# A transformer's three one-unit cross attentions: order of VectorE's steps and of one ScalarE copy in a unit

## What is computed

```python
x = x + _L0_xattn_ref(_layernorm(x), ctx_512, ...)    # cross attention, 16 heads of 8
x = x + _L0_ffn_ref(_layernorm(x), ...)               # experts
x = x + _L1_xattn_ref(_layernorm(x), ctx_512, ...)    # causal self attention + cross attention
x = x + _L1_ffn_ref(_layernorm(x), ...)               # experts
x = x + _L2_xattn_ref(_layernorm(x), ctx_512, ...)    # two attentions with 16 heads of 32
x = x + _L2_ffn_ref(_layernorm(x), ...)               # experts
x = x + _L3_xattn_ref(_layernorm(x), ctx_512, ...)    # cross attention, 16 heads of 8
x = x + _L3_ffn_ref(_layernorm(x), ...)               # ternary MLP
```

```python
q, k, v = layernorm(x) @ Wq, ctx @ Wk, ctx @ Wv       # 256 queries, 64 keys, 16 heads of 8
x = x + (softmax(q @ k.T / sqrt(8)) @ v) @ Wo + bo
```

## Time and profile before

| | |
|---|---|
| median of 3 runs | 2486.17 us (2484.84 to 2491.94) |
| the profiled execution, device time | 2488.64 us |
| its span, first to last instruction | 2486.9 us |
| PE busy | 2136.2 us, 86% |
| PEld busy (weight load) | 1629.6 us, 66% |
| DVE busy | 1824.4 us, 73% |
| ACT busy | 1335.7 us, 54% |
| POOL busy | 1247.5 us, 50% |
| mean granted TensorE clock | 0.946 |

### The profile page before, as it was taken

One profiled execution on the slowest core, in us unless ns is written; L12 is line 12 of the kernel. 1 busy time (PEld: TensorE's weight loads), 2 busy tenths in 40 slices (PEclk: granted clock), 3 DMA queues, 4 the chain that ended last, 5 costly groups with the idle time before them and its releaser, 6 DMA issues. The chain is left out here.

```text
span 2486.9 us, 67321 instructions
## 1 busy us (share of the span) xinstructions
PE 2136.2 (86%) x22352; PEld 1629.6 (66%) x22352; DVE 1824.4 (73%) x4650; ACT 1335.7 (54%) x2821; POOL 1247.5 (50%) x1940
## 2 busy tenths in 40 slices
PE   5878997999988779599999997899789999998755
PEld 4557995556656568466666666666567888875523
DVE  5975554666659766489999968688698866667887
ACT  2444552444434456355555547355468888873466
POOL 4547635555535366477777745333264343334333
PEclk9978998999999879799999999899999999999978
DMA  8022211000000223200000000000000312210000
GB/s 307 20 112 76 78 53 30 16 13 14 11 2 1 83 76 105 62 13 11 9 9 11 8 2 21 10 1 0 19 5 2 103 56 67 56 43 15 1 11 24
DMA packets 82031, 96.69 MB, mean 39 GB/s; under 512 B 16720, under 2 KB 61136, under 8 KB 79760
## 3 DMA queue, kind: packets, MB, share of 16 engines
q1 hardware_dynamic: 73616, 77.12, 9.9%
q0 software_dynamic: 8192, 16.79, 2.3%
HBM read 56.51 MB, written 37.36 MB: 38 GB/s over the span
## 5 line engine op out<-in xcount | busy, mean ns | idle before, releaser
L1722 DVE TENSOR_TENSOR l2f_h_lo<-l2f_h,l2f_h_hi 128x512 fp32r<-128x512 f32 x256 | 187.1, 763 | 101.1 <-ACT l2f_h_hi L1643 101.0
L1012 POOL TENSOR_TENSOR a_pm<-a_pt,tri_post 128x256 f32<-128x256 f32 x256 | 179.6, 731 | 71.8 <-ACT a_pt L668 71.4
L1650 ACT ACTIVATE l2f_h<-l2f_f,ahead 128x512 f32<-128x512 f32 x256 | 174.2, 688 | 49.6 <-DVE l2f_h_lo L1722 32.5
L808 DVE TENSOR_REDUCE l1s_negm<-l1s_s 128x6 bf16<-128x768 f32 x128 | 123.1, 961 | 95.7 <-PE l1s_s L485 95.5
L1817 POOL TENSOR_TENSOR l2f_acc<-l2f_tmp,l2f_acc 128x512 f32<-128x512 f32 x56 | 73.0, 1303 | 207.2 <-DVE l2f_tmp L1740 207.2
L668 ACT ACTIVATE l1s_pt<-l1s_st 128x768 f32<-128x768 f32 x128 | 96.9, 812 | 144.9 <-PE l1s_st L523 144.9
L808 DVE TENSOR_REDUCE a_negm<-a_s 128x4 bf16<-128x1024 f32 x128 | 156.2, 1220 | 23.2 <-PE a_s L485 23.1
L1643 ACT ACTIVATE l2f_h_hi<-l2f_h 128x512 fp32r<-128x512 f32 x256 | 154.4, 633 | 0.0
L668 ACT ACTIVATE a_pt<-a_st 128x1024 f32<-128x1024 f32 x128 | 126.6, 1066 | 3.3 <-PE a_st L523 3.3
L684 ACT ACTIVATE a_q_hi<-a_pa 128x256 bf16<-128x256 f32 x64 | 24.5, 383 | 184.7 <-PE a_pa L451 184.7
L1534 PE MATMUL l2f_f<-l2f_x_hi,l2f_w_hi 128*128 128x512 f32 x256 | 101.7, 397 | 1.2 <-POOL l2f_w_lo L1804 1.2
(11 more groups left out here) (575 smaller groups left out, 6930.1 us busy)
## 6 DMA issues: line engine op xcount, KB each, us to landing
expert_rows<-zeros SPq DMA_DIRECT2D x16, 1056.0 KB, 17.5
l2f_wrow<-weights_by_expert SPq DMA_DIRECT2D x64, 256.0 KB, 3.2
l0f_w<-in_l0f_w SPq DMA_DIRECT2D x8, 640.0 KB, 9.7
l0f_x_in_sb<-expert_rows SPq DMA_DIRECT2D x72, 64.0 KB
expert_rows<-l0f_y SPq DMA_DIRECT2D x72, 64.0 KB, 1.6
l1f_x_in_sb<-expert_rows SPq DMA_DIRECT2D x72, 64.0 KB
expert_rows<-l1f_y SPq DMA_DIRECT2D x72, 64.0 KB
ahead<-in_l2f_w SPq DMA_DIRECT2D x6, 512.0 KB, 4.6
```

The costliest lines, as they stand in the source:

```text
L808: dve.tensor_reduce(dst, src, AX.X, ALU.max, negate=True).then_inc(max_done, 1)
L1012: last = pool.tensor_tensor(pm[:, par, heads_, kt, :], pt[:, par, heads_, kt * (T + P):kt * (T + P) + P], K["tri_post"][:].unsqueeze(1).br ...
L1650: act.activation(h[:, j], psum_f[j][:], ACT.Gelu, bias=col(e, j)).then_inc(h_ready, 1)
L1722: dve.tensor_tensor(h_lo[:, pos % 2, j], h[:, j], h_hi[:, pos % 2, j].bitcast(F32), ALU.subtract)\
```

## The change

Two orders are changed, in the stages with U = 1 only. On VectorE the residual of n-2 and the second maxima of n+1 now come right behind the first maxima, and `ln_apply(n+3)` and `ln_stats(n+4)` follow behind them (the new function `norms_of` holds the loop that stood there). On ScalarE the copy of the turned tokens stands between the two exponentials. The orders of TensorE, GpSimd and SyncE are the same as before.

```diff
@@ ScalarE, emit
                 if inside(n):
                     exps(n, pos, 0)
+                if U == 1 and inside(n2):
+                    turned(b2)
+                if inside(n):
                     exps(n, pos, 1)
                 if U == 4 and inside(nn) and (per_unit or un == 0):
                     copy_v(nn, bn, un, posn)
-                if inside(n2) and u2 == 0:
+                if U == 4 and inside(n2) and u2 == 0:
                     turned(b2)
@@ VectorE
+            def norms_of(at, kinds):
+                for when, what, i in sorted(plan, key=lambda p: (-p[0], p[2])):
+                    na, ba, ua, posa = at(LEAD - when)
+                    if inside(na) and ua == 0 and what in kinds:
+                        if what == "merge":
+                            merge_choice(ba, (posa // U) % 2, i)
+                        elif what == "stats":
+                            ln_stats(ba, i)
+                        else:
+                            ln_apply(ba, i)
+
...
                 if inside(nn):
                     maxima(nn, posn, 0)
-                for when, what, i in sorted(plan, key=lambda p: (-p[0], p[2])):
-                    na, ba, ua, posa = at(LEAD - when)
-                    if inside(na) and ua == 0:
-                        if what == "merge":
-                            merge_choice(ba, (posa // U) % 2, i)
-                        elif what != "gather":
-                            ln_stats(ba, i) if what == "stats" else ln_apply(ba, i)
+                if U == 4:
+                    norms_of(at, ("merge", "stats", "apply"))
                 residual_now = inside(nw) and uw == U - 1 and store_t is None
                 if residual_now and inside(nn):
                     residuals(bw)
@@
                     maxima(nn, posn, 1)
                     if before:
                         join_maxima(nn, posn)
+                if U == 1:
+                    norms_of(at, ("stats", "apply"))
                 if paired and U == 1 and inside(n1):
                     turn_sums(n1, n1)
```

## The result

The changed kernel takes **2528.14 us** (median of 4 runs, 2527.38 to 2535.03) against 2486.62 us for the kernel before (4 runs, 2484.84 to 2491.94): ratio **1.017**, 95% interval 1.0146 to 1.0193. It is slower by 41.5 us. I had forecast +23.4 us, 2509.6, with a range of 2500 to 2522: the direction is right, the size too small, and the time lies outside the range.

What follows compares the result with a forecast made beforehand. VectorE was taken to bound the old loops, a closed chain through GpSimd's keys the new. Chain +27.8, head -2.85, copy's wait -1.5 gave +23.4 us, median 2509.6; range 2500 to 2522 (2500 to 2519 for the forecast alone).

Steps and rivals of the forecast that it cites:

- VectorE sets the pace before, GpSimd's order decides after: Loops: VectorE, busy 93%, bounds the old step; afterwards GpSimd's late keys close a chain longer than VectorE's 6.96 us.
- M1: VectorE's second maxima of a step, taken as zero; the chain runs from one to the next.
- The sum of the chain: Links from second maxima to second maxima: 7.77, 8.18, 7.20 us a step in l0, l1c, l3; together +27.8 us.
- end of `mv` to `kb_hi`: Chain link on GpSimd, without a pause: 1.77 us with the preset (l0, l1c), 1.20 without it (l3).
- projection to residual: Chain link from TensorE's output projection to VectorE's residual: 0.91 us, 1.32 in l1c with twice the matmuls.
- `kb_hi` to scores: Chain link from GpSimd's keys to the first half of TensorE's scores that waited for them: 0.92 us.
- keys are held up: Rival: kb_hi waits for a VectorE multiplication, up to 0.47 us a step, 15.5 us, time up to 2525; chance 0.10.
- TensorE's clock falls: Rival: idling 1.7 us a step lowers TensorE's clock, at most 73 us, near 2560 with 1.5 us a step; chance 0.03.
- Head and tail: Outside the chain: second maxima earlier in step 1, -2.85 us; no wait for the copy in step 13, -1.5 us.
- ScalarE's copy costs nothing: ScalarE: the second exponential moves back by one copy at no cost; the projection no longer waits for the copy.
- VectorE only: Rival: GpSimd's wait is absorbed, the step is VectorE's 6.96 us, 2484.7 us, no change; chance 0.05.
- faster: Rival: VectorE's multiplications no longer meet GpSimd, 0.5 us instead of 0.94, 14.5 us less, 2470; chance 0.03.

Runs made afterwards that it cites:

- e3: Changed kernel with GpSimd taking the keys ahead of the deviations and the preset in stages with U = 1: 2488.52 us, ratio 0.9898 to the kernel before.
- e8: Changed kernel with only GpSimd's preset moved behind the keys, the deviations staying ahead of them: 2505.64 us, ratio 1.0087 to the kernel before.
- e4: Changed kernel with 20 small identity matmuls per step filling TensorE's gap between turn and scores: 2545.9 us, ratio 1.0134 to the kernel before.
- e5: Kernel before with only GpSimd's keys taken ahead of the deviations and the preset in stages with U = 1: ratio 0.9989 to the kernel before.
- e1: Changed kernel with ScalarE's copy put back behind both exponentials, VectorE's new order kept: 2552.2 us, ratio 1.0161 to the kernel before.
- e2: Kernel before with only ScalarE's copy of the turned tokens moved between the two exponentials: 2503.29 us, ratio 0.997 to the kernel before.

## Why the prediction was right in direction and wrong in size

- **VectorE sets the pace before, GpSimd's order decides after: right.** `kb_hi` waits for `mv` through deviations and preset, the scores for `kb_hi`, M1 for the scores. e3 breaks the first link and the loss is gone; e8 takes out one link, and the step shortens by 0.65 us, about its length.
- **The sum of the chain: a little short.** Forecast 7.77 / 8.18 / 7.20 us, measured without the clock's part (e4) 7.87 / 8.32 / 7.20, which over the steps is +30.3 us where I had +27.8. The terms that missed are small: end of `mv` to `kb_hi` 1.87 instead of 1.77, because the preset, now beside `on_t`, took 0.73 instead of 0.64 us; projection to residual 1.02 instead of 0.91; and, the other way, `kb_hi` to scores 0.80 instead of 0.92. That is all that the rival "keys are held up" has to it, 0.1 us a step of the 0.47 it might have been. GpSimd's instructions got longer by a tenth and started on time. VectorE paid more: `on_t` takes 0.94 us beside GpSimd's work and 0.49 without it (e3). The row below is the second multiplication of the step shown in full above. It starts while the preset runs, takes 0.73 us where it takes 0.29 in e3, and ends 0.15 us behind the preset. In the kernel before the pair ends just as closely behind `kb_f`, at 60.78 against 60.64. The exclusion that the Trainium skill (SBUF — State Buffer, the section on two separate sides) states, for whichever of the two comes second, fits these rows. So the trace does not speak against the rule; what was too high was my price for GpSimd, 0.47 us, where it lost 0.09 on the preset and 0.05 on `kb_hi`.

```profile
92.30 0.73 DVE L831 TENSOR_TENSOR l_on_t<-l_nd_t,l_rec_nd 128x128 f32<-128x128 f32 x1
```

- **The step that failed is the chance and the term of the rival "TensorE's clock falls".** It had a chance of 0.03, and the sum of the forecast had no term for it. It lengthened 13 of 33 steps and cost 12.7 us, two thirds of the 18.5 us by which the time lies above the forecast. The rest is 2.5 of the chain, 1.5 of head and tail, and 1.8 because the profiled execution lay 2.5 us above the median before and only 0.7 above it after. I had the gap (1.7 us forecast, 1.60 measured) and the price of a fall (up to 1.5 us a step; 0.5 to 1.6 measured). What was wrong was the argument against it: 72% busy at clock 0.99 at the end of `l3`. That stretch says little about a gap of 1.6 us: up to 2356.8 us it has none longer than 0.75. The same trace has gaps of 1.32 us in the first steps of `l0`, and one of them shows a fall. The timeline of the kernel before, then its busy time by stretch:

```profile
42.14 0.39 PE L485 MATMUL l_s<-l_kb_hi,l_q_hi 32*128 32x256 bf16 x2 [1.32 <-DVE l_negm L808]
...
2356.13 0.68 PE L611 MATMUL l_pa<-ahead,l_o_t 128*128 128x128 f32 x4 [0.75 <-DVE tokens_x L877]
```

```profile
41.00:42.00 1.00, 0.00 (x0) 0.00 (x0) 1.00 (x2) 1.00 (x2) 0.01 (x1) 1.00 1.06 439
43.00:44.00 1.00, 1.00 (x16) 0.73 (x8) 0.87 (x3) 0.00 (x0) 0.34 (x2) 0.50 1.03 431
```

The clock is 1.00 in the gap and 0.50 behind it. So the trace that the prediction was made from already held a reason to give the rival more than 0.03. A mean busy share told nothing here: in the changed kernel one stretch of 15 us with 11.72 us busy had clock 1.00 and another with 12.36 had 0.89, and the lower clock itself makes the matmuls longer and so the share higher. The Trainium skill (TensorE: Matmul & The Clock Gate, on oscillation) warned of idling between bursts; here the trace agrees with it, with falls behind gaps of 1.6 us, though the pauses in the page's main example are longer. I also treated the rival as all or nothing, 2560 or no effect. A fall in every second or third step was a case of its own. With what the runs show now it would have been 0.4 x 33 steps x 1 us = 13 us, 2523 as its middle, and the range would have reached 2528.
- **The bounds were added up wrong.** 2509.6 with 5 us either way and the spread of -1.3 to +5.7 gives 2503 to 2520, not 2500 to 2519. Neither reaches 2528.
- **Head and tail: -4.35 forecast, -2.8 measured** for everything outside the three loops together. It can't be held against the terms of the forecast: the clock in the first steps of a stage changes from run to run (0.89 and 0.78 before in `l0` and `l1c`, 1.00 in e5), and in those two stages the first two steps took 3.6 and 3.1 us more before than in e5.
- **ScalarE's copy costs nothing: right, for the wrong comparison.** e1 and the changed kernel are alike. But alone it gains 0.3% (e2). The prediction said that the projection no longer waits for the copy, and didn't say that this half would pay without the other.
- **"VectorE only", 6.96 us a step, and "faster", 2470: too long a step, though its condition was right.** With the keys early (e3) the step is 6.4 us in `l0`, mostly since the multiplications no longer meet GpSimd, which is the condition that I had put into the rival "faster". I had taken it to be against GpSimd's order, and without a further edit it is.

What stays open: e4's filled gap changes two things at once, the idle stretch and TensorE's busy share. So the runs show what the clock costs, 12.7 us in steps 1 to 12, and not which of the two brings it down. Nor do they show why it held behind 3 of the 15 long gaps, or why in e8 it fell behind gaps of 0.97 and 1.19 us, where in the changed kernel it held behind 18 such steps. In e3, some 5 us of the gain between the medians (21.2 us) lie outside what the column "all" has (16.3). The profiled execution of e3 is its slowest, 2496.46 us against a median of 2488.52, which can account for it; the faster ones have no trace.

## What to carry to other kernels

Before an instruction is put later on one engine, ask which in-order queue has an instruction that waits for it, and what stands behind that one: here the norm statistics, needed three steps later, stood ahead of keys needed at once. Putting the urgent work first in that queue turned a loss of 1.7% into a gain of 1.0% (0.8% by the medians). When a sum opens a new idle stretch on TensorE in each step, look in the trace at hand for gaps of that length and for the granted clock behind them, not for a stretch with the same mean busy share, and give a fall in some of the steps a case of its own with its price.

## What the runs showed of the hardware

- The granted clock of TensorE fell from 1.00 to 0.50 behind 12 of 15 idle stretches of 1.35 to 1.61 us in steps 1 to 12 of the changed kernel, and in none of the 18 steps with a shorter one. In e1 it fell behind 11 of 16 and 0 of 17, in e8 behind the one of 1.42 us and in 2 of the other 32 steps (0.97 and 1.19 us). In the step shown it stayed low for 3.4 us of unbroken work and came back. A fall shortened the next gap in 8 of 11 cases; in `l1c` four falls came in a row. 20 small matmuls in the gap (1.28 us of work a step) prevented it. They cost no visible time in steps 1 to 12, where TensorE had nothing to do there, but the first and last steps of the stages were 6.2 us longer with them.
- VectorE's multiplications with two operands in SBUF (`on_t`, two of 128x128 f32) take 0.94 us beside GpSimd's 128x256 instructions and 0.49 us with only `veps` (128x2) beside them; the second of the two ends 0.15 us behind the GpSimd instruction that it met. The norm's scaling goes from 402 ns in the mean (the kernel before, where it meets `vb`) to 339 (changed kernel) and 340 (e3). GpSimd's partner instructions lengthen only from 0.61 to 0.66 (`kb_hi`) and from 0.64 to 0.73 us (preset). The engine that loses most by such a meeting is VectorE.
